# Conditioned residual pair on one core: all stores by pairs of 8 KB rows, loads left in fours

## The chip, the cores and the metric

The kernel runs on one core of one Trainium2 chip. The metric is the device time of one execution in microseconds (us). It is read as the median of several executions; profiles come from one more execution, which is recorded by the hardware profiler.

## The reference

There are 128 batches, each a matrix of 128 channels by 1024 time steps in float32. Two layers are applied to each. The first adds a product with one of 200 weight matrices, the second adds a product with one of 8 and a bias of 128 values:

```python
def _L0_cond_ref(x, conditions, weights):
    w = weights[conditions]
    return jnp.einsum('bct,bcd->bdt', x, w)
...
def _L1_cond_ref(x, subjects, weights, bias):
    w = weights[subjects]
    b = bias[subjects]
    out = jnp.einsum('bct,bcd->bdt', x, w)
    out = out + b[:, :, None]
    return out
x = x + _L0_cond_ref(x, itok_B_1_198, L0_cond_weights)
x = x + _L1_cond_ref(x, itok_B_0_7, L1_cond_weights, fside_8xS_0)
```

So out = (I + W1)^T (I + W0)^T x + b for each batch. The kernel reads x once and writes out once: 67.1 MB each way.

## The kernel before

The kernel forms one 128x128 matrix m = (I + W0)(I + W1) for each batch on TensorE, sums its parts on VectorE (`sum_m`), and multiplies it with x in two halves of 512 columns each (`results`). VectorE evicts the left half from PSUM with the bias added (`left`, line 378), ScalarE the right half (`right`, line 402). Both write back into the tile `xy`, over the x that has been used.

`xy` holds a ring of 8 slots. A slot is a pair of batches (2 x 1024 floats, 8 KB in each partition). Two slots make a "quad", four batches, and the ring holds four quads (QUAD = 2 slots, QUADS = 4). The 128 batches are 64 pairs, so the ring is filled 8 times (ROUNDS = 8). In DRAM, x and out are laid out by quads with the channel outermost: one channel of a quad is 16 KB in one piece, a channel of a pair is 8 KB of it.

The transfers of x and out are issued by SyncE (SP), in an order written out by hand, and all pass through the SP queue:

- at the start the first two pairs are loaded as pairs, then quads 1 to 3 (`load_quad`, lines 176 to 183), mixed with the loads of the first W0 matrices (64 KB each, rows of 512 B);
- `store_pair` stores slots 0 to 3 one by one, with `load_quad_again(1, 0)` among them (lines 188 to 192);
- then a loop (lines 193 to 199) has for each quad: the W0 loads of the quad after next (`load_w0_of`), the store of a finished quad (`store_quad`, line 156), and the load of a new one (`load_quad_again`, line 166), which first waits until the store that emptied its quad of the ring has landed. That store was issued one step of the loop earlier, so a store and a load are queued behind it whenever SP keeps up;
- the last part (lines 201 to 221) does the same without the loop, loads the last pair in smaller pieces, and stores quads 1 and 2 of the last round with `store_quad`, the pair after them with `store_pair`, and the last pair in halves of a batch, the left ones from SP, the right ones from ScalarE's queue (line 417).

`store_quad` waits in `wait_out` for the second pair of the quad, which is evicted after the first, and then issues one DMA of 2 MB. `store_pair` waits for its one pair and issues 1 MB. Each DMA adds 16 to the semaphore `stored[q]` of its quad. `stored_once(r, q)` is the value that says that quad q has been stored r times; for the first two quads it holds 16 more, since they were stored in two pieces in round 0. SP waits for it in `load_quad_again`, GpSimd ahead of `pick` (line 272; it copies the matrices of each batch from their home into the places that TensorE reads), and ScalarE at the end (line 420).

Of the kernel before, what the change touches and what calls it, by code (L numbers as in the profile page):

```python
# [11 lines left out]
def conditioned_residual_kernel(nc, x, cond, w0_t, w1_bias, out):  # L12
# [11 lines left out]
    NQ, C, QB, T = x.shape  # L24
    B = NQ * QB
    N0, _, D = w0_t.shape
    N1 = w1_bias.shape[1]
    assert C == D == 128
    PAIR = 2
    RING = 8  # L30
    QUAD = QB // PAIR
    QUADS = RING // QUAD
    PAIRS = B // PAIR
    ROUNDS = PAIRS // RING
# [3 lines left out]
    MB = 2  # L38
    YB = 2
    AHEAD = QUADS - 1  # L40
    BY_PAIR = 2
    assert PAIRS % RING == 0 and HALF <= 512 and RING % MB == 0 and ROUND_B % YB == 0

    with ExitStack() as ctx:
        def sb(name, shape, dt=F32):
            return ctx.enter_context(nc.sbuf_tensor(name, shape, dt))

        def sem(name):
            return ctx.enter_context(nc.semaphore(name))


        xy = sb("xy", [C, RING, PAIR, T])
# [35 lines left out]
        stored = [sem(f"stored{q}") for q in range(QUADS)]  # L88
# [12 lines left out]
        def half(h):  # L101
            return slice(h * HALF, (h + 1) * HALF)

        def slots(q):
            return xy[:, q * QUAD:(q + 1) * QUAD, :, :].rearrange("c s k t -> c (s k t)")

        def quad_of(t, r, q):
            return t[bass.ds(r * QUADS + q, 1), :, :, :].rearrange("n c k t -> (n c) (k t)")
# [3 lines left out]

        def stored_once(r, q):

            return r * 16 + (16 if q < BY_PAIR else 0)

        block = ctx.enter_context(nc.Block())

# [1 line left out]
        def _(sp):  # L120
# [29 lines left out]
            def wait_out(r, s):  # L150
                for k in range(PAIR):
                    b = s * PAIR + k
                    sp.wait_ge(left_out[b % YB], r * (ROUND_B // YB) + (b // YB + 1))  # L153
                    sp.wait_ge(right_out[b % YB], r * (ROUND_B // YB) + (b // YB + 1))  # L154

            def store_quad(r, q):

                wait_out(r, q * QUAD + QUAD - 1)
                sp.dma_start(quad_of(out, r, q), slots(q)).then_inc(stored[q], 16)  # L159

            def store_pair(r, s):
                wait_out(r, s)
# [3 lines left out]
            def load_quad_again(r, q):  # L166
                sp.wait_ge(stored[q], stored_once(r, q))
                load_quad(r, q)
# [24 lines left out]
            with sp.Fori(1, ROUNDS - 1) as r:  # L193
                for q in range(1, QUADS + 1):
                    now = (r, q) if q < QUADS else (r + 1, 0)
                    after = (r, q + 1) if q + 1 < QUADS else (r + 1, q + 1 - QUADS)
                    load_w0_of(*after)
                    store_quad(*((r, q - AHEAD) if q >= AHEAD else (r - 1, q - AHEAD + QUADS)))
                    load_quad_again(*now)

            for q in range(1, QUADS):
                if q < QUADS - 1:
                    load_w0_of(ROUNDS - 1, q + 1)
                store_quad(*((ROUNDS - 1, q - AHEAD) if q >= AHEAD else (ROUNDS - 2, q - AHEAD + QUADS)))
                if q < QUADS - 1:
                    load_quad_again(ROUNDS - 1, q)

            sp.wait_ge(stored[QUADS - 1], stored_once(ROUNDS - 1, QUADS - 1))
            load_pair(NQ - 1, LAST - 1, x_loaded[QUADS - 1])
            for k in range(PAIR):  # L210
# [3 lines left out]
            for q in range(1, QUADS - 1):  # L214
                store_quad(ROUNDS - 1, q)
# [10 lines left out]
        def _(pool):  # L226
            def pick(r, s):


                pool.wait_ge(w0_loaded[s], r * (PAIR * 16) + PAIR * 16)  # L230
                _, words = nc.values_load_multi_w_load_instructions(
                    pick_words[0:1, bass.ds(r * ROUND_B + s * PAIR, PAIR), :].rearrange("o b f -> o (b f)"),
                    engines=(mybir.EngineType.Pool,),
                    skip_runtime_bounds_check_because="each word is checked against its own range below")
                for k in range(PAIR):
                    home = nc.s_assert_within(words[2 * k], 0, B - 1)
                    i = nc.s_assert_within(words[2 * k + 1], 0, N1 - 1)
                    nc.gpsimd.tensor_copy(w0_pick[:, s, k, :],  # L238
                                          w0_home[:, bass.ds(home, 1), :].rearrange("k b c -> k (b c)"))
                    last = nc.gpsimd.tensor_copy(  # L240
                        j_pick[:, s, k, :], j_all[:, bass.ds(i, 1), :].rearrange("c n d -> c (n d)"))
                last.then_inc(picked, 1)

            def pick_first(s):


                _, words = nc.values_load_multi_w_load_instructions(
                    cond_words[0:1, 1, s * PAIR:(s + 1) * PAIR], engines=(mybir.EngineType.Pool,),
                    skip_runtime_bounds_check_because="each word is checked against its own range below")
                for k in range(PAIR):  # L250
                    i = nc.s_assert_within(words[k], 0, N1 - 1)
                    last = nc.gpsimd.tensor_copy(  # L252
                        j_pick[:, s, k, :], j_all[:, bass.ds(i, 1), :].rearrange("c n d -> c (n d)"))
                last.then_inc(picked, 1)
# [14 lines left out]
            with pool.Fori(1, ROUNDS) as r:  # L269
                for s in range(RING):  # L270

                    pool.wait_ge(stored[s // QUAD], stored_once(r, s // QUAD))
                    pick(r, s)
# [120 lines left out]
        @block.scalar  # L394
        def _(act):
            def right(r, s, k):

                b = s * PAIR + k
                if k == 0:
                    act.wait_ge(picked, r * RING + (s + 1))  # L400
                act.wait_ge(y_ready, r * (2 * ROUND_B) + (2 * b + 2))
                nc.scalar.activation(xy[:, s, k, half(1)], y_ps[:, b % YB, 1, :], ACT.Identity,  # L402
                                     bias=j_pick[:, s, k, D:D + 1]).then_inc(right_out[b % YB], 1)

            act.dma_start(cond_words[:].rearrange("o f b -> o (f b)"), cond).then_inc(cond_loaded, 16)
            with act.Fori(0, ROUNDS - 1) as r:
                for s in range(RING):
                    for k in range(PAIR):
                        right(r, s, k)
            for s in range(RING - 1):  # L410
                for k in range(PAIR):
                    right(ROUNDS - 1, s, k)
            for k in range(PAIR):
                b = LAST * PAIR + k
                right(ROUNDS - 1, LAST, k)
                act.wait_ge(right_out[b % YB], (ROUNDS - 1) * (ROUND_B // YB) + b // YB + 1)
                act.dma_start(out[NQ - 1, :, QB - PAIR + k, half(1)], xy[:, LAST, k, half(1)]).then_inc(last_stored, 16)
            for q in range(QUADS):

                act.wait_ge(stored[q], stored_once(ROUNDS, q))  # L420


# [23 lines left out]
```

## Time and profile before

| | |
|---|---|
| median of 3 runs | 347.63 us (347.43 to 348.22) |
| time of the profiled execution | 348.84 us |
| its span, first to last instruction | 347.1 us |
| busy share: TensorE matmul / VectorE / ScalarE / GpSimd | 77% / 36% / 28% / 19% |
| DMA packets, bytes, mean rate | 24058, 140.80 MB, 406 GB/s |
| share of 16 DMA engines taken by SP's queue | 97.9% |

Busy share is the time in which an engine ran instructions that count as work; the rate is what the 16 DMA engines of the core moved. "Issue to landing" is the time from SP's DMA instruction to the end of the whole transfer, with the time that it waited behind earlier ones.

### The profile page before, as it was taken

The page shows a single profiled execution, that of the slowest core. Times are in us where ns is not written, and L with a number is a line of the kernel's source. Part 1 is how long each engine was busy: PE and PEld are TensorE (multiplying, and loading weights), DVE is VectorE, ACT ScalarE, POOL GpSimd, SP SyncE. Part 2 cuts the span into 40 slices and gives each one's busy share as a digit, 9 for nine tenths or more (in the row PEclk, how much of TensorE's full clock was granted, in tenths as well). Part 3 has the DMA queues.
Part 4 walks back from the last instruction along what each step waited for, and adds up shares of the span by engine and source line. Part 5 has one row for each costly group of instructions (what it writes and reads, how often), then busy time and mean ns, then how long its engine had stood idle before and what let it go on. Part 6 is the DMA issues. An engine that isn't in the chain of part 4 may idle for free.

```text
span 347.1 us, 5157 instructions
## 1 busy us (share of the span) xinstructions
PE 266.8 (77%) x774; PEld 129.5 (37%) x774; DVE 126.3 (36%) x202; ACT 96.9 (28%) x135; POOL 65.3 (19%) x249
## 2 busy tenths in 40 slices
PE   1799991986798896979877779777679877778980
PEld 1344450442344442434433334433334433333430
DVE  3254541333334242433433344333334333334440
ACT  1133350221333133332232232422242222323230
POOL 2400222112221112221122212122221212221000
PEclk9999997899989898998999999999999999999996
DMA  7999969999999999999999999999999999999994
GB/s 306 410 409 393 378 248 351 424 418 397 417 431 415 433 423 427 417 416 427 432 425 427 427 423 432 421 436 423 419 431 425 432 430 426 423 421 440 419 405 171
DMA packets 24058, 140.80 MB, mean 406 GB/s; under 512 B 2673, under 2 KB 14322, under 8 KB 15474
## 3 DMA queue, kind: packets, MB, share of 16 engines
q1 hardware_dynamic: 23760, 140.20, 97.9%
q10 hardware_dynamic: 290, 0.53, 0.4%
q14 instruction: 7, 0.06, 0.0%
q8 instruction: 1, 0.02, 0.0%
HBM read 76.03 MB, written 67.11 MB: 412 GB/s over the span
## 4 chain that ended last, share of the span: by engine, by line
DMA 56%; SPq 27%; issue 9%; PE 5%; ACT 0%
DMA out<-xy 47%; SPq L127 10%; DMA xy<-x 9%; SPq L122 7%; PE y_ps L306 5%; SPq L128 4%; SPq L142 3%; SPq L145 2%; ACT xy L402 0%; PE m_ps L287 0%; SPq L159 0%; SPq L148 0%; SPq L153 0%; SPq L163 0%; SPq L154 0%
## 5 line engine op out<-in xcount | busy, mean ns | idle before, releaser
L306 PE MATMUL y_ps<-xy,m_sb 128*128 128x512 f32 x512 | 245.5, 616 | 61.3 <-DMA xy<-x 60.3
L306 PEld LDWEIGHTS y_ps<-xy,m_sb 128*128 128x128 f32 x512 | 92.9, 196 | 164.9 <-issue 164.9
L402 ACT ACTIVATE xy<-y_ps,j_pick 128x512 f32<-128x512 f32 x128 | 87.9, 687 | 233.1 <-PE y_ps L306 233.1
L378 DVE TENSOR_SCALAR xy<-y_ps,j_pick 128x512 f32<-128x512 f32 x128 | 96.1, 751 | 156.5 <-PE y_ps L306 156.5
L238 POOL COPY w_pick<-w_home 128x128 f32 x112 | 32.8, 293 | 245.4 <-issue 245.4
L287 PEld LDWEIGHTS m_ps<-j_pick,w_pick 128*128 128x128 f32 x224 | 35.4, 199 | 28.7 <-issue 28.7
L370 DVE TENSOR_TENSOR m_sb<-m_ps,j_pick 128x256 f32<-128x256 f32 x64 | 27.1, 424 | 45.2 <-PE m_ps L287 44.6
L287 PE MATMUL m_ps<-j_pick,w_pick 128*128 128x128 f32 x224 | 35.1, 281 | 0.0
L240 POOL COPY j_pick<-j_all 128x129 f32 x112 | 33.0, 295 | 0.1
L402 ACT ACT_TABLE_LOAD x7 | 9.0, 1283 | 7.9 <-POOL j_pick L252 7.8
L287 PE MATMUL m_ps<-j_pick,w_home 128*128 128x128 f32 x32 | 5.5, 297 | 6.7 <-DMA w_home<-w_t 6.7
L287 PEld LDWEIGHTS m_ps<-j_pick,w_home 128*128 128x128 f32 x32 | 5.3, 212 | 10.6 <-issue 10.4
L252 POOL COPY j_pick<-j_all 128x129 f32 x16 | 4.7, 295 | 10.3 <-issue 9.9
L312 PE MATMUL cond_ps<-cond_row,ones 1*128 1x128 f32 x2 | 0.8, 481 | 2.4 <-DVE cond_row L341 2.4
L344 DVE TENSOR_TENSOR j_all<-j_all,eye 128x1024 f32<-128x1024 f32 x1 | 1.2, 1226 | 2.3 <-DMA j_all<-w_bias 2.3
L361 DVE TENSOR_TENSOR load_words<-home_ps,batch_less_b 1x128 int32<-1x128 f32 x1 | 0.3, 278 | 4.7 <-PE home_ps L320 4.7
L312 PEld LDWEIGHTS cond_ps<-cond_row,ones 1*128 1x128 f32 x2 | 0.5, 309 | 2.4 <-issue 2.4
L341 DVE CAST cond_row<-cond_words 1x128 f32<-1x128 int32 x1 | 0.2, 214 | 2.1 <-DMA cond_words<-cond 2.1
L320 PE MATMUL home_ps<-eye,home_less_b 128*1 128x128 f32 x2 | 0.6, 394 | 0.0
L313 PEld LDWEIGHTS cond_ps<-ones,cond_row 1*128 1x128 f32 x2 | 0.5, 330 | 0.0
L313 PE MATMUL cond_ps<-ones,cond_row 1*128 1x1 f32 x2 | 0.4, 277 | 0.0
L351 DVE TENSOR_SCALAR same<-cond_ps,cond_col 128x128 f32<-128x128 f32 x1 | 0.4, 351 | 0.0
(16 smaller groups left out, 2.8 us busy)
## 6 DMA issues: line engine op xcount, KB each, us to landing
xy<-x SPq DMA_DIRECT2D x30, 2048.0 KB, 15.1
out<-xy SPq DMA_DIRECT2D x29, 2048.0 KB, 13.4
w_home<-w_t SPq DMA_DIRECT2D x128, 64.0 KB
out<-xy SPq DMA_DIRECT2D x5, 1024.0 KB, 6.8
xy<-x SPq DMA_DIRECT2D x3, 1024.0 KB, 7.8
xy<-x SPq DMA_DIRECT2D x4, 256.0 KB, 12.6
j_all<-w_bias SPq DMA_DIRECT2D x1, 516.0 KB, 3.7
out<-xy SPq DMA_DIRECT2D x2, 256.0 KB, 5.1
```

The source lines that it names most:

```text
L122: return nc.values_load_multi_w_load_instructions(words, engines=(mybir.EngineType.SP,), skip_runtime_bounds_check_because="each word is c ...
L127: sp.dma_start(w0_home[:, bass.ds(b, 1), :].rearrange("k b c -> k (b c)"), w0_t[bass.ds(nc.s_assert_within(i, 0, N0 - 1), 1), :, :].rearra ...
L128: w0_t[bass.ds(nc.s_assert_within(i, 0, N0 - 1), 1), :, :].rearrange("n k c -> (n k) c"),
L142: load_one(b + k, s, words[2 * k], nc.s_assert_within(words[2 * k + 1], 0, 1))
L145: sp.dma_start(slots(q), quad_of(x, r, q)).then_inc(x_loaded[q], 16)
L238: nc.gpsimd.tensor_copy(w0_pick[:, s, k, :], w0_home[:, bass.ds(home, 1), :].rearrange("k b c -> k (b c)"))
L240: last = nc.gpsimd.tensor_copy(j_pick[:, s, k, :], j_all[:, bass.ds(i, 1), :].rearrange("c n d -> c (n d)"))
L287: last = nc.tensor.matmul(m_ps[:, s % MB, k * D:(k + 1) * D], w0_of_k, j_pick[:, s, k, 0:D], start=True, stop=True)
L306: nc.tensor.matmul(y_ps[:, b % YB, h, :], m_sb[:, s, k, :], xy[:, s, k, half(h)], start=True, stop=True).then_inc(y_ready, 1)
L370: nc.vector.tensor_tensor(m_sb[:, s, :, :], m_ps[:, s % MB, 0:PAIR * D].rearrange("c (k d) -> c k d", k=PAIR), j_pick[:, s, :, 0:D], ALU.a ...
L378: nc.vector.tensor_scalar(xy[:, s, k, half(0)], y_ps[:, b % YB, 0, :], j_pick[:, s, k, D:D + 1], None, ALU.add).then_inc(left_out[b % YB], 1)
L402: nc.scalar.activation(xy[:, s, k, half(1)], y_ps[:, b % YB, 1, :], ACT.Identity, bias=j_pick[:, s, k, D:D + 1]).then_inc(right_out[b % YB ...
```

## The change

`store_quad` no longer issues one DMA of rows of 16 KB after the second pair is evicted. It goes through the two slots of its quad; for each it waits for that slot's pair and issues a DMA of 1 MB with rows of 8 KB. The semaphore of a quad now rises by 32 in each round, so `stored_once` becomes `r * 32` for every quad, and ScalarE's last wait is for 16 less on the last quad, whose last pair is stored in halves that count on another semaphore. Loads, the W0 loads, and the order of the issues are as before.

```diff
-    BY_PAIR = 2
...
         def stored_once(r, q):
 
-            return r * 16 + (16 if q < BY_PAIR else 0)
+            return r * (QUAD * 16)
...
             def store_quad(r, q):
 
-                wait_out(r, q * QUAD + QUAD - 1)
-                sp.dma_start(quad_of(out, r, q), slots(q)).then_inc(stored[q], 16)
+                for s in range(q * QUAD, (q + 1) * QUAD):
+                    wait_out(r, s)
+                    sp.dma_start(out[bass.ds(r * QUADS + q, 1), :, (s % QUAD) * PAIR:(s % QUAD + 1) * PAIR, :]
+                                 .rearrange("n c k t -> (n c) (k t)"),
+                                 xy[:, s, :, :].rearrange("c k t -> c (k t)")).then_inc(stored[q], 16)
...
             for q in range(QUADS):
 
-                act.wait_ge(stored[q], stored_once(ROUNDS, q))
+                act.wait_ge(stored[q], stored_once(ROUNDS, q) - (16 if q == QUADS - 1 else 0))
```

## Rows read from the trace of the kernel before

**Rows 1.** The page: 40 slices of DMA share (tenths) and rate; SP's queue.
```profile
DMA  7999969999999999999999999999999999999994
GB/s 306 410 409 393 378 248 351 424 418 397 417 431 415 433 423 427 417 416 427 432 425 427 427 423 432 421 436 423 419 431 425 432 430 426 423 421 440 419 405 171
...
q1 hardware_dynamic: 23760, 140.20, 97.9%
```

**Rows 2.** DMA issues: transfer, issuing queue, count, KB each, median us from issue to landing.
```profile
xy<-x SPq DMA_DIRECT2D x30, 2048.0 KB, 15.1
out<-xy SPq DMA_DIRECT2D x29, 2048.0 KB, 13.4
...
out<-xy SPq DMA_DIRECT2D x5, 1024.0 KB, 6.8
```

**Rows 3.** SP's waits, 60 to 300 us: total us, times, longest; none other there.
```profile
SPq L145 <- DMA out<-xy: 55.6, 23, 3.5
```

**Rows 4.** Timeline of SP, two steps of the loop: start us, us, line, transfer.
```profile
74.17 0.35 SPq L159 DMA_DIRECT2D out<-xy  x1
77.71 0.35 SPq L145 DMA_DIRECT2D xy<-x  x1
80.01 4.96 SPq L127 DMA_DIRECT2D w_home<-w_t  x4
85.40 0.35 SPq L159 DMA_DIRECT2D out<-xy  x1
88.17 0.35 SPq L145 DMA_DIRECT2D xy<-x  x1
```

**Rows 5.** Timeline of ACT there: the last eviction of one quad.
```profile
79.72 0.69 ACT L402 ACTIVATE xy<-y_ps,j_pick 128x512 f32<-128x512 f32 x1 [1.48 <-PE y_ps L306]
```

**Rows 6.** Windows: stretch, us, five engines' busy time, granted clock, DMA share, GB/s.
```profile
0.00:28.00 28.00, 17.89 (x51) 9.42 (x52) 9.99 (x21) 5.41 (x7) 5.76 (x25) 1.00 0.95 369
...
28.00:34.00 6.00, 6.00 (x22) 3.13 (x21) 3.06 (x6) 2.06 (x3) 0.00 (x0) 1.00 1.02 422
...
30.00:34.00 4.00, 4.00 (x14) 1.98 (x13) 2.04 (x4) 1.37 (x2) 0.00 (x0) 1.00 1.02 424
...
200.00:300.00 100.00, 78.46 (x237) 37.72 (x236) 38.12 (x60) 30.05 (x42) 20.46 (x78) 1.00 1.01 427
...
306.00:318.00 12.00, 9.53 (x32) 4.72 (x31) 4.77 (x8) 3.40 (x5) 2.12 (x8) 1.00 1.04 433
...
312.00:322.00 10.00, 7.51 (x25) 3.60 (x24) 3.85 (x6) 2.75 (x4) 2.12 (x8) 1.00 0.99 424
```

**Rows 7.** Chain of work, first store of the loop: start us, us, line.
```profile
47.43 0.06 SPq L153
...
47.83 0.36 SPq L159
```

**Rows 8.** Timeline of SP at the start of the loop, and windows there.
```profile
26.88 1.88 SPq L163 DMA_DIRECT2D out<-xy  x3
...
57.15 0.35 SPq L159 DMA_DIRECT2D out<-xy  x1
...
46.00:48.00 2.00, 2.00 (x9) 1.21 (x8) 0.75 (x1) 1.97 (x3) 1.06 (x4) 1.00 0.13 38
```

**Rows 9.** The end: SP's waits from 300 us, timelines of SP and ACT, windows.
```profile
SPq L153 <- DVE xy L378: 14.0, 3, 9.1
...
320.22 10.83 SPq L159 DMA_DIRECT2D out<-xy  x2
...
326.06 0.69 ACT L402 ACTIVATE xy<-y_ps,j_pick 128x512 f32<-128x512 f32 x1 [1.42 <-PE y_ps L306]
...
326.00:328.00 2.00, 2.00 (x9) 1.04 (x8) 0.75 (x1) 0.69 (x1) 0.00 (x0) 1.00 1.16 483
...
330.00:332.00 2.00, 2.00 (x9) 1.12 (x8) 0.75 (x1) 0.91 (x2) 0.00 (x0) 1.00 0.94 396
...
342.00:344.00 2.00, 0.00 (x0) 0.00 (x0) 0.00 (x0) 0.00 (x0) 0.00 (x0) 0.50 0.12 49
```

## The prediction

> **What bounds the kernel now.** I read the slices of the page first [rows 1]. From the seventh slice to the last but one the DMA share stands at nine tenths or more, and the rate at 397 to 440 GB/s from the eighth on, while TensorE is busy for 77% of the span and no other engine for more than 36%. SP's queue alone took 97.9% of the time of 16 DMA engines. So the transfers are the bound; the reader should see that there is one real hole in the middle (slice 6, at 248 GB/s) and a thin last slice (171). The issues come second [rows 2]: a 2 MB load lands 15.1 us after its issue and a 2 MB store 13.4 us after, though 2 MB at 427 GB/s [rows 6] take only 4.9 us. The rest is waiting behind earlier transfers: about 4 MB lie ahead of each. Third come SP's own waits [rows 3]: between 60 and 300 us it waits only at line 145, for the landing of the store that frees a quad, 23 times, 2.4 us each. Its timeline [rows 4] shows the same: store issued at 85.40, then idle until the store of 74.17 has landed, load at 88.17. A step takes 88.17 - 77.71 = 10.5 us, which is 4.19 MB of x and out and up to 0.26 MB of W0 at 427 GB/s (10.4 us). SP is paced by the transfers, not the transfers by SP.
>
> **Part 1, the wait is split so that a pair can leave earlier.** In the loop this moves nothing. The quad that SP stores at 85.40 [rows 4] had its last eviction at 79.72 + 0.69 = 80.41 us [rows 5], 5.0 us before. SP arrives late because it issues W0 loads from 80.01 to 84.97. Both pairs are long evicted, and the two DMAs will go out back to back. None of SP's waits from 60 to 300 us is for an eviction [rows 3]. Value 0, and no gain in the loop, since even a store issued earlier would stand in a queue that is full.
>
> **Part 2, the price of the extra issue on SP.** The first store of the loop shows the whole step [rows 7]: from 47.43 us (the first wait's register work) to 48.19 us (the end of the issue), 0.76 us, with the address arithmetic. The change adds one such step to each quad store, about 0.8 us. It stands ahead of the wait for landing at line 145, which has 2.4 us of idle time in the mean [rows 3] and some 2.3 us in the step shown (85.75 to about 88.0) [rows 4]. Cover: that idle time. Behind SP are queued the load and the next W0 loads; neither is delayed, as the landing of the older store sets the load's issue. The second half of a store gets into the queue 0.8 us later, with some 10 us of transfers ahead of it. Value 0. If the cover were gone it would be 24 x 0.8 = 19 us in the loop. The loads' own wait is for the same bytes as before, in the same place in the queue; the higher count at lines 145, 272 and 420 moves nothing.
>
> At the start of the loop there is less cover. The queue runs dry at 46 to 48 us (38 GB/s, share 0.13) [rows 8], because SP is late, and stays thin until the next store at 57.15 us. The dry spell itself ends with the first store, which still goes out at about 47.8 us, and its 1 MB (2.5 us at 422 GB/s) covers the 0.8 us until the second. The next store would then be at 57.15 + 0.8 = 58.0 us. From about 48.1 us the queue holds 4.19 + 0.26 = 4.45 MB, 10.5 us, so until 58.6 us. It just holds, with 0.6 us to spare. The bounds are 0 and one step of SP, 0.8 us (no gain is possible where SP arrives late); I take a quarter of the step, **+0.2 us**, as the margin is as small as the step.
>
> **Part 3, the rows of 8 KB.** This is the term that matters, as it sits on the bound itself. There are 29 quad stores [rows 2], so 29 x 2.097 = 60.8 MB go by 8 KB rows: 29 x 128 = 3712 rows of 16 KB become 7424, and 29 more DMAs complete. The trace has one stretch that is made of such stores and nothing else. By 26.9 us SP had issued the joint table (0.5 MB), two pairs (2.1), three quads (6.3) and up to 20 W0 matrices (1.3), together 10.2 MB; 28 us at 369 GB/s are 10.3 MB [rows 6]. So at 28 us those are done, and the three 1 MB stores issued from 26.88 to 28.76 [rows 8] are what moves from 28 to 34 us: 422 GB/s at a share of 1.02 [rows 6]. The hundred microseconds of the loop, all 16 KB rows but for the W0, move 427 GB/s [rows 6]. Then 60.8 MB take 60.8 / 0.422 = 144.1 us in place of 60.8 / 0.427 = 142.4 us: **+1.7 us**. The 28 to 34 stretch holds three completions, so they are in that price. Bounds: the shorter cut 30 to 34 (424) against the stretch 312 to 322 (424), where no W0 is left: 0. And 422 against 306 to 318 (433): 144.1 - 140.4 = +3.7 us. I take 1.7, from the two longest and cleanest windows, though W0 rows slow the 427 a little, which speaks for more rather than less.
>
> Here the Trainium skill has a rule that speaks against the change. "DMA: Bandwidth & Descriptors", section "Why small descriptors are slow (HBM only)", gives each packet three cycles on top of one per 32 bytes. By that 8 KB cost 259 and 16 KB 515 cycles, so two halves 518 for 515, 0.6% of 142 us; an estimate of +0.8 us by that page, and the sum would be 1.0 us in place of 1.9. The trace's own rates ask for somewhat more.
>
> **Part 4, the end.** Here SP does wait for evictions, 14.0 us in 3 waits [rows 9]: before the stores of the last round. The store at 331.05 - 0.35 = 330.7 us (quad 2, the second of the two at 320.22 [rows 9]) could send its first pair when ScalarE has evicted it, at 326.06 + 0.69 = 326.75 us: 1 MB leaves SP 3.9 us earlier. But the engines are full all that time: 483 GB/s at 326 to 328 us, 396 at 330 to 332, shares 1.16 and 0.94 [rows 9]. What is issued earlier only queues earlier. Value 0. Below nothing the bound is the time that the last engines work nearly alone: from 342 us the share is 0.12 [rows 9], for some 3 us to the end, a tail that another order could shorten by at most 3 us. On the other side an extra issue of 0.8 us before the last stores. There I take 0 all the same, as SP is waiting for an eviction ahead of each of these stores and has the time.
>
> **Sum.** 0 (part 1) + 0.2 (part 2) + 1.7 (part 3) + 0 (part 4) = 1.9 us. On the profiled execution that is 348.84 + 1.9 = 350.7 us (span 347.1 + 1.9 = 349.0). The profiled execution lies 1.2 us above the median of the runs, which is what counts: 347.63 + 1.9 = **349.5 us**.
>
> **The rivals.**
> (a) *No change.* The rows of 8 KB move at the rate of 16 KB ones, as the pair 424 and 424 says [rows 6], and everything else is covered: 347.6 us, 347.0 to 348.3. A 6 us window is short, and in its favour is that a few GB/s is what single windows differ by. Against it: the DMA share is full, so nothing hides even a small price.
> (b) *Faster.* The end has slack of its own: the early first pair of quad 2 (3.9 us ahead) and of quad 1 in the last round fills some engines that would otherwise be empty, and the stretch of thin work after 342 us shrinks. It gives up to 3 us less the 1.7 us, so about 346.3 us. It decides only if some engines run dry before 331 us; the shares of 1.16 and 0.94 speak against that.
> (c) *Much slower: SP becomes the bound.* If the added step costs more than the 2.4 us of cover [rows 3], or the queue empties once again after 57 us and does not refill, each dry step costs up to 0.8 us. Four of them before the queue is full again are 3.2 us, which with the 1.7 is 347.63 + 4.9 = 352.5 us. It decides when the queue's 10.5 us of bytes fall short of SP's step.
> (d) *Each DMA has a fixed part that isn't hidden.* A 1 MB store lands 6.8 us after its issue [rows 2] with at most two such stores (5.0 us) ahead of or in it, so 1.8 us is fixed. If that were on the path 29 times it would be 52 us, 400 us in all. The stretch of three in a row at 422 GB/s rules it out almost wholly. The Trainium skill, same page, section "Bandwidth", has figures of this kind (transfers of 1 MB issued from GpSimd reach 341 GB/s, of 16 MB 425); the trace's 422 GB/s at 1 MB, queued from SP, disagrees.
>
> **How the numbers follow.** About 0.2% (0.7 us) is what a measurement of this kernel can tell from no change. The forecast (cost of 0.7 to 3.7 us, 348.3 to 351.3) has 0.62, (a) 0.20, (b) 0.12, (c) 0.05, (d) 0.01. Slower is the forecast with (c) and (d), 0.68; same is (a), 0.20; faster is (b), 0.12. The range goes from 347.0, the lower end of (a), to 351.3, the upper end of the forecast, 0.82 by these cases.
>
> **What would show it.** Packets rise by 3712 rows and 29 x 16 = 464 completions to about 28,230, at the same 140.8 MB; the rate from 200 to 300 us falls from 427 to some 423 to 425 GB/s at an unchanged share; SP's wait at line 145 (its new number) shrinks from 2.4 to about 1.6 us each; two store issues stand 0.8 us apart in each step, both after the evictions; the hole before the first store of the loop stays as it is; in the last round one store leaves near 327 + 2 us and changes nothing. I am wrong if the rate in the loop does not fall, if the hole at 46 us widens or a second one appears after 57 us, or if the thin stretch at the end changes its length by over a microsecond.

## The result and the profile after

| | before | changed |
|---|---|---|
| median of 5 runs | 347.63 us (347.41 to 348.22) | 350.74 us (350.16 to 351.35) |
| ratio, 95% interval | | 1.0086 (1.0067 to 1.0105) |
| profiled execution, span | 348.84 us, 347.1 us | 351.13 us, 349.3 us |

The changed kernel is 3.1 us slower; by the interval 2.3 to 3.7 us. The page of its profile, with the same lines as [rows 1] and the span and packets with them:

```profile
span 349.3 us, 5304 instructions
...
DMA  7999969999999999999999999999999999999984
GB/s 306 412 401 394 356 243 363 436 417 426 407 420 420 426 432 419 417 418 426 421 433 429 416 425 425 423 421 434 431 417 425 424 429 422 432 420 421 415 335 185
DMA packets 28235, 140.81 MB, mean 403 GB/s; under 512 B 3137, under 2 KB 14786, under 8 KB 15938
...
q1 hardware_dynamic: 27936, 140.20, 97.6%
```

The same bytes go in 4177 more packets; the hole in slice 6 is as it was (243 for 248 GB/s), the loop's slices are alike, and the last slice but one is thinner: 335 for 405 GB/s. The issues, to be held against [rows 2] (columns as there):

```profile
out<-xy SPq DMA_DIRECT2D x63, 1024.0 KB, 9.6
xy<-x SPq DMA_DIRECT2D x30, 2048.0 KB, 15.0
```

SP's one wait from 60 to 300 us (as [rows 3]), and its timeline at the start of the loop and in two later steps (as [rows 4]; line 159 is the store, line 144 the load):

```profile
SPq L144 <- DMA out<-xy: 38.5, 20, 3.0
...
48.28 1.08 SPq L159 DMA_DIRECT2D out<-xy  x2
49.57 1.11 SPq L144 DMA_DIRECT2D xy<-x  x1
...
58.15 1.07 SPq L159 DMA_DIRECT2D out<-xy  x2
59.42 1.16 SPq L144 DMA_DIRECT2D xy<-x  x1
...
68.35 1.07 SPq L159 DMA_DIRECT2D out<-xy  x2
69.63 0.84 SPq L144 DMA_DIRECT2D xy<-x  x1
...
106.84 1.07 SPq L159 DMA_DIRECT2D out<-xy  x2
110.47 0.35 SPq L144 DMA_DIRECT2D xy<-x  x1
```

Two stores stand where one stood and take 1.08 us together, 0.73 more than one. The wait behind them has shrunk as it should, over the 23 loads of the stretch; but three of these loads found no wait at all. In the changed kernel the first five loads of the loop (49.57 to 89.82 us) leave 0.2 us behind the stores, in the kernel before only the first two (48.46 and 57.70 us). And the load takes SP 1.11 and 1.16 us in the first steps, where one of before took 0.34 to 0.35 [rows 4]. Windows, columns as in [rows 6], first of the changed kernel, then two that the section of rows did not need, of the kernel before:

```profile
0.00:60.00 60.00, 44.20 (x130) 22.72 (x130) 22.70 (x41) 16.31 (x22) 11.97 (x48) 0.99 0.92 354
60.00:110.00 50.00, 40.36 (x106) 19.58 (x107) 16.59 (x26) 12.97 (x18) 8.85 (x34) 0.88 1.02 422
...
200.00:300.00 100.00, 79.46 (x240) 38.31 (x239) 38.21 (x60) 29.37 (x41) 20.31 (x76) 1.00 1.01 425
...
324.00:328.00 4.00, 3.90 (x9) 2.24 (x10) 0.75 (x1) 0.69 (x1) 0.00 (x0) 0.61 1.02 399
345.00:348.00 3.00, 0.00 (x0) 0.00 (x0) 0.00 (x0) 0.00 (x0) 0.00 (x0) 0.55 0.07 26
```

```profile
0.00:60.00 60.00, 43.44 (x130) 22.20 (x130) 22.70 (x41) 16.31 (x22) 12.19 (x49) 0.98 0.92 355
60.00:110.00 50.00, 41.35 (x117) 20.24 (x118) 18.08 (x28) 13.93 (x20) 8.54 (x33) 0.93 1.02 419
```

Two things are to be seen. In the loop the rate is 425 for 427 GB/s. And by 110 us the changed kernel has moved no less than the one before: 0.354 x 60 + 0.422 x 50 = 42.34 MB for 0.355 x 60 + 0.419 x 50 = 42.25 MB. Yet its load of that time is issued at 110.47 us, the other's at 109.07. A load goes out when the whole of an older store has landed, so it waits for the last of the 16 DMA engines, and the mean rate does not show that one. The last window shows it alone: 26 GB/s at a share of 0.07 is one engine of 16 at full speed (427 / 16 = 26.7), still at work three microseconds after the others.

The trace shows the same within the loop, as it has the time of each of the 16 additions to a semaphore. For the load issued at 88.17 us (89.82 in the changed kernel) the fifteenth comes at 103.35 us before and at 103.11 us in the changed kernel, the last at 103.62 and at 105.07 us: it trails by 0.3 and by 2.0 us. In the second profile of each, below, it trails by 0.0 and by 2.6 us.

**Where the time went.** The starts of the loads of x are the clock of this kernel, so they date the loss. Each column is one profiled execution; the second of each kernel comes from the experiments below.

| load issued, us | before | before again | changed | changed again | means differ by |
|---|---|---|---|---|---|
| first after the pair stores | 34.16 | 33.83 | 34.91 | 33.85 | +0.4 |
| first of the loop | 48.46 | 48.34 | 49.57 | 49.02 | +0.9 |
| seventh of the loop | 109.07 | 108.52 | 110.47 | 110.45 | +1.7 |
| last quad | 306.24 | 305.75 | 307.87 | 307.75 | +1.8 |
| last pair | 316.82 | 316.30 | 319.04 | 318.92 | +2.4 |
| end of the span | 347.1 | 346.6 | 349.3 | 349.3 | +2.5 |

The 0.4 us at 34 us lies ahead of the first changed instruction and is chance. Of the other 2.1 us, 0.5 arise at the first doubled store, 0.8 in the next 60 us, 0.1 in the 200 us after that, and 0.6 between the last two loads. Three experiments below came out as the kernel before once more. Against the mean of all five such profiles the last column reads +0.3, +0.8, +1.8, +2.2, +2.8 and +2.8 us, so the 200 us of the loop lose 0.4 us and not 0.1.

### The profile page after: what moved, and what is told of

Same layout as the page of the kernel before. It is cut to its first block, busy times and chain, and to the rows that moved or that the text cites. A ratio compares the mean times of both kernels' runs of the same rounds, so it can differ in the third digit from the quotient of the medians.

```text
span 349.3 us, 5304 instructions
## 1 busy us (share of the span) xinstructions
PE 269.9 (77%) x774; PEld 131.1 (38%) x774; DVE 126.2 (36%) x202; ACT 97.0 (28%) x135; POOL 65.7 (19%) x249
## 2 busy tenths in 40 slices
DMA packets 28235, 140.81 MB, mean 403 GB/s; under 512 B 3137, under 2 KB 14786, under 8 KB 15938
## 4 chain that ended last, share of the span: by engine, by line
DMA 59%; SPq 21%; PE 9%; issue 8%; DVE 1%; ACT 1%
DMA out<-xy 34%; DMA xy<-x 25%; PE y_ps L308 8%; SPq L126 7%; SPq L121 5%; SPq L127 3%; SPq L141 2%; SPq L159 2%; SPq L144 2%; PE m_ps L289 1%; DVE xy L380 1%; ACT xy L404 1%; SPq L152 0%; SPq L147 0%; SPq L165 0%
## 5 line engine op out<-in xcount | busy, mean ns | idle before, releaser
L289 PEld LDWEIGHTS m_ps<-j_pick,w_pick 128*128 128x128 f32 x224 | 36.2, 203 | 29.9 <-issue 29.9
L289 PE MATMUL m_ps<-j_pick,w_pick 128*128 128x128 f32 x224 | 35.9, 285 | 0.0
```

Of the source, the lines that this page charges most:

```text
L289: last = nc.tensor.matmul(m_ps[:, s % MB, k * D:(k + 1) * D], w0_of_k, j_pick[:, s, k, 0:D], start=True, stop=True)
```

## The experiments

All ratios are to the kernel before, run beside each kernel on the same chip. The microseconds behind a ratio are that ratio of some 347.8 us; medians subtracted from each other can differ from them by half a microsecond. Most lines of an edit that only follow from those shown are left out.

**The changed kernel again.** No edit.

> The changed kernel once more, unaltered, for a second profile and a second ratio. Theory R (the price lies on the rows of 8 KB, spread evenly over the loop, about 1.7 us): ratio near 1.005 to 1.009, and from the issue at 109 us to that at 307 us the loads of x fall behind the kernel before by over 1.0 us. Theory S (the price lies at the two ends of the program, where SP is late at the start of the loop and where the last quads are computed, and the loop itself costs nearly nothing): same ratio, but over those 19 quads the loads fall behind by under 0.4 us, and from the last loads to the last eviction by over 1.0 us. If the first profile's hole at 338 us and TensorE's clock of 0.50 at 326 us were chance, they are gone here and the span is shorter by 1 to 2 us.

Measured: 350.50 us, ratio 1.0064 (1.0041 to 1.0086), +2.2 us; span 349.3. From the load near 109 us to that near 307 us its lag on the first profile of before went from 1.38 to 1.51 us: 0.13 us over 19 quads (0.23 in the first profile), as S said and not R. That test is weaker than it looks: five profiles of the kernel before take 196.3 to 197.2 us for these quads, and the two of the changed kernel 197.4 and 197.3. The 1.0 us that S put behind the last loads isn't there. The late last product of the first profile was chance. The chain of the second, and the timeline of the first, at the quad after the last full load:

```profile
323.98 1.96 PE y_ps L308 x4
```

```profile
324.11 3.02 PE L308 MATMUL y_ps<-xy,m_sb 128*128 128x512 f32 x4 [3.14 <-DMA xy<-x]
```

In the first, TensorE had idled 3.14 us and ran at a granted clock of 0.61 in the mean from 324 to 328 us (a mix of its two levels, 1.2 and 2.4 GHz), so its last eviction began at 341.13 us, in the second at 339.33. Both spans are 349.3. The end is set by the last DMA engine, not by the last product.

**Pairs in the loop alone.**

Against the changed kernel; the counts of `stored_once` follow, and GpSimd's last round is taken out of its loop:

```diff
+    IN_LOOP = 2
+    AFTER_LOOP = 1
...
-            def store_quad(r, q):
-
+            def store_quad(r, q, n=AFTER_LOOP):
+                if n == 1:
+                    wait_out(r, q * QUAD + QUAD - 1)
+                    sp.dma_start(quad_of(out, r, q), slots(q)).then_inc(stored[q], 16)
+                    return
                 for s in range(q * QUAD, (q + 1) * QUAD):
...
-                    store_quad(*((r, q - AHEAD) if q >= AHEAD else (r - 1, q - AHEAD + QUADS)))
+                    store_quad(*((r, q - AHEAD) if q >= AHEAD else (r - 1, q - AHEAD + QUADS)), n=IN_LOOP)
```

> Stores by pairs only in the 24 quads of SP's loop; the five quads stored behind the loop go as one DMA of 2 MB each again. GpSimd's last round is taken out of its loop so that the counts can differ. Theory R: 24/29 of the cost stays, +2.6 us of the measured +3.1. Theory S: what is left is the start of the loop, +0.5 to +1.4 us, and the last stretch from the loads of the last pair to the end is as in the kernel before (no share under 0.8 between 330 and 340 us). Rival N (the end is set by noise in when the last loads land, whatever form the stores have): ratio as the changed kernel's.

Measured: 350.59 us, ratio 1.0063 (1.0044 to 1.0082), +2.2 us (1.5 to 2.8). With 24 of the 29 quads the whole of the cost is there within the intervals. R's +2.6 us lies in the interval, S's +0.5 to +1.4 us does not; from 330 to 340 us no window of 2 us falls under a share of 0.89, as S said. But the profile of this kernel is 0.8 us late before any store (its load at 6.7 us goes out at 7.54), and if all its executions are, that is part of its 2.2 us.

**Pairs behind the loop alone.** The same code with `IN_LOOP = 1` and `AFTER_LOOP = 2`.

> Stores by pairs only in the five quads stored behind SP's loop; the 24 in the loop go as one DMA of 2 MB each. GpSimd's last round is taken out of its loop as well. Theory R: 5/29 of the cost, +0.5 us, ratio 1.001 to 1.002. Theory S: +1.0 to +2.0 us, ratio 1.003 to 1.006, with the last eviction more than 1 us later than in the kernel before although the loads up to 306 us are issued at the same times as there (within 0.4 us).

Measured: 348.74 us, ratio 1.0025 (1.0006 to 1.0044), +0.9 us (0.2 to 1.5). Small, but not nothing. The profile can't place it, since the profiled execution took 351.28 us, the slowest of the kernel's twelve, and it too is late from the start (7.60 for 6.72 us). R's +0.5 us lies in the interval, S's upper half does not; the last eviction is late (339.05 us), but the load at 306 us of before is late by 1.81 us there as well, so that test of S could not be made.

**Two DMAs with rows of 16 KB.**

```diff
-                sp.dma_start(quad_of(out, r, q), slots(q)).then_inc(stored[q], 16)
+                for p in (slice(0, C // 2), slice(C // 2, C)):
+                    sp.dma_start(out[bass.ds(r * QUADS + q, 1), p, :, :].rearrange("n c k t -> (n c) (k t)"),
+                                 xy[p, q * QUAD:(q + 1) * QUAD, :, :].rearrange("c s k t -> c (s k t)"))\
+                      .then_inc(stored[q], 16)
```

> All 29 quads are stored in two DMAs of 1 MB as in the changed kernel, but cut by partitions (64 and 64) with rows of 16 KB, both issued after the second pair is evicted. So the second issue and the second completion stay, and the rows of 8 KB and the early first pair are gone. Theory R: the cost goes, ratio 0.999 to 1.002. Theory S with SP's second issue as the cause at the start: the loads at 59 and 69 us are late as in the changed kernel (1.7 and 3 us behind before), and at least +1 us stays. If it is slower than the changed kernel, 64 partitions use the engines less evenly, and it tells nothing of rows.

Measured: 376.88 us in the median of five executions, ratio 1.0827 (1.0777 to 1.0876), +29 us; the profiled one took 382.81 us, the longest. It answers another question: two DMAs of 64 partitions take longer here than one of 128, with the same rows. Its page and its loop:

```profile
DMA packets 24523, 140.81 MB, mean 370 GB/s; under 512 B 3137, under 2 KB 14786, under 8 KB 15938
...
200.00:300.00 100.00, 77.76 (x218) 37.53 (x217) 34.91 (x55) 27.30 (x38) 19.12 (x72) 0.94 1.00 389
```

The share is full at 389 GB/s, so packets took longer: rows of 16 KB 667 ns in the mean of this stretch, for 612 before. It tells nothing of the change.

**The kernel before again.** No edit.

> The kernel before, unaltered, as a second profile: how far two executions of the same program stand apart stage by stage. If its loads are issued within 0.3 us of the first profile's, then the +1.4 us by which the changed kernel's loads are late at 109 us is the change's; if they differ by 1 us, the start varies by itself and less can be read from it. Ratio 1.000 within 0.002.

Measured: 347.85 us, ratio 0.9991 (0.9972 to 1.0011). Its loads stand 0.1 to 0.6 us from those of the first profile (table above). So differences under about half a microsecond between two profiles say nothing (under one microsecond, with the three further profiles below), and the changed kernel's 1.7 us at 109 us does.

**GpSimd's loop cut, nothing else.** The control for the two kernels with pairs in one part.

```diff
-            with pool.Fori(1, ROUNDS) as r:
+            with pool.Fori(1, ROUNDS - 1) as r:
+                pick_round(r)
+            pick_round(ROUNDS - 1)
```

> The kernel before with only GpSimd's last round taken out of its loop, as the two kernels with pairs in one part had it. Both had their second load of x 0.8 to 0.9 us late already at 6.7 us, ahead of any store. If the longer GpSimd program is the cause, it shows here too: loads at 6.7 to 34 us late by 0.8 to 1.4 us, and a ratio of 1.001 to 1.003, which has to be taken off theirs: the pairs in the loop then cost 0.4 to 0.6%, and the pairs behind it 0 to 0.2%. If not, it is 1.000.

Measured: 347.83 us, ratio 0.9997 (0.9979 to 1.0014); its loads up to 16 us are within 0.02 us of before's. The cut costs nothing by itself. But the late start of the two kernels above (there SP waited 0.9 and 1.0 us for its index words) isn't here, so this control does not cover it. Whether it was in all their executions, and so in their ratios, is open. The 0.9 us of the pairs behind the loop could be mostly that.

**One DMA with rows of 8 KB, first try.**

```diff
-                sp.dma_start(quad_of(out, r, q), slots(q)).then_inc(stored[q], 16)
+                sp.dma_start(out[bass.ds(r * QUADS + q, 1), :, :, :].rearrange("n c (s k) t -> (n c) s (k t)", s=QUAD),
+                             xy[:, q * QUAD:(q + 1) * QUAD, :, :].rearrange("c s k t -> c s (k t)"))\
+                  .then_inc(stored[q], 16)
```

> Each quad is stored by one DMA once both pairs are evicted, as in the kernel before, but its access pattern is split so that a row is 8 KB: the rows of the change without its second issue, second completion and early first pair. Packets near 27,800. Theory R (rows): ratio 1.005 to 1.008. Theory S (SP's second issue delays the start, the tail does the rest): 0.999 to 1.002.

Measured: 347.89 us, ratio 0.9997 (0.9980 to 1.0013), but the packets line shows that the edit did not take:

```profile
DMA packets 24058, 140.80 MB, mean 406 GB/s; under 512 B 2673, under 2 KB 14322, under 8 KB 15474
```

24058 is the number of before. The two pieces, adjoining on both sides, were joined to rows of 16 KB. It is one more run of the kernel before.

**SP's time alone.**

```diff
                 sp.dma_start(quad_of(out, r, q), slots(q)).then_inc(stored[q], 16)
+                words_of(load_words[0:1, 0:PAIR, :].rearrange("o b f -> o (b f)"))
```

> The kernel before, with one more read of index words into SP's registers behind each quad store (0.5 to 0.9 us of SP's time, nothing else): SP's added time of the change alone, without rows or DMAs. Theory S: the loads at 59 to 70 us fall 1 to 3 us behind, and the ratio is 1.003 to 1.006. Theory R: the wait for the landing at the load swallows it, ratio 0.999 to 1.001.

Measured: 347.78 us, ratio 1.0000 (0.9983 to 1.0017), and this too is void: the profile holds 5157 instructions, as before. The words are not used, so the read was presumably dropped. SP's time by itself stays untried.

The two void kernels serve as further profiles of the kernel before; with the first two and that of the cut loop there are five. Their loads near 109 us stand at 107.99 to 109.40 us, those of the last quad at 305.09 to 306.24 us. The changed kernel's, at 110.46 and 307.81 us in the mean, lie 1.1 and 1.6 us behind the latest of them. Their rate from 200 to 300 us is 426 to 428 GB/s, the changed kernel's 425 in both profiles: a small fall, but a real one (summed packet by packet, 42.67 to 42.73 MB for 42.54 and 42.50).

**Rows of 8 KB in all loads and stores, no further issue.**

```diff
-        xy = sb("xy", [C, RING, PAIR, T])
+        xy_wide = sb("xy", [C, RING, PAIR * T + 64])
+        xy = xy_wide[:, :, 0:PAIR * T].rearrange("c s (k t) -> c s k t", k=PAIR)
...
-            return xy[:, q * QUAD:(q + 1) * QUAD, :, :].rearrange("c s k t -> c (s k t)")
+            return xy[:, q * QUAD:(q + 1) * QUAD, :, :].rearrange("c s k t -> c s (k t)")
...
-            return t[bass.ds(r * QUADS + q, 1), :, :, :].rearrange("n c k t -> (n c) (k t)")
+            return t[bass.ds(r * QUADS + q, 1), :, :, :].rearrange("n c (s k) t -> (n c) s (k t)", s=QUAD)
```

> The kernel before with 256 B of room behind each pair in the ring of x, so that the 16 KB of a quad are no longer one piece in SBUF: each of its rows has to go as two of 8 KB, in loads and stores alike, still one DMA for each quad. Packets near 31,600, no second issue, no second completion. It carries twice the rows of the change. Theory R (8 KB rows cost 1.7 us for the stores): +3.5 us or more, ratio near 1.010. Theory S (rows cost nearly nothing in the loop; the changed kernel's loads fell behind there by only 0.13 and 0.23 us over 19 quads): 0 to +1 us, ratio under 1.003.

Measured: 351.73 us, ratio 1.0100 (1.0080 to 1.0120), +3.5 us (2.8 to 4.2). The edit took this time (packets), and SP's issues grew a little longer with it, from 0.35 to 0.6 us:

```profile
DMA packets 31611, 140.80 MB, mean 402 GB/s; under 512 B 2674, under 2 KB 14323, under 8 KB 15475
...
78.55 0.64 SPq L160 DMA_DIRECT2D out<-xy  x1
79.47 0.60 SPq L146 DMA_DIRECT2D xy<-x  x1
```

Twice the rows of the change cost what R said. Half of it, 1.7 us (1.4 to 2.1), would be the stores' part if loads and stores weigh alike. The time that the DMA engines were at work gives the price without the ratio. It stands on the pages, as SP's queue's share of the span; of the changed kernel's second profile, and of this kernel:

```profile
q1 hardware_dynamic: 27936, 140.20, 97.7%
```

```profile
q1 hardware_dynamic: 31312, 140.20, 97.9%
...
200.00:300.00 100.00, 78.23 (x238) 37.99 (x238) 37.37 (x59) 29.67 (x42) 20.14 (x76) 1.00 1.02 424
```

Before, 97.9% of 347.1 us are 339.8 us for each engine. In the changed kernel it is 340.9 and 341.3 us, here 343.0 us: 1.1 to 1.5 us for the rows of the stores, completions included, and 3.2 us for those of all quads. Single packets agree: most rows of 16 KB take 611 ns and most of 8 KB 309 ns, so two halves take 7 ns more, and 3712 x 7 ns / 16 engines = 1.6 us. The remaining rows of 16 KB were not slower in the changed kernel (619 and 620 ns in the mean, for 618 to 620 in the five profiles of before). The rate of the loop falls with it, 427 before, 425 changed, 424 here.

The starts of the loads are a poorer measure. At 34 us they are already 1.49 us late (35.65 for 34.16), from first loads which the change leaves alone, and from the first load of the loop (50.22 for 48.46, +1.76) to that of the last quad (309.36 for 306.24, +3.12) they fall behind by 1.36 us over 25 loads and as many stores: 0.8 us for 29 stores, 1.4 against the fastest of the five profiles of before. So the rows of the change are worth some 1.1 to 1.6 us, and at most 2.1.

**One small DMA more behind each quad store.**

```diff
+            def one_more(q):
+                sp.dma_start(spare[:, q, :], w0_t[0, 0:16, :]).then_inc(spared[q], 16)
...
                 sp.dma_start(quad_of(out, r, q), slots(q)).then_inc(stored[q], 16)
+                sp.wait_ge(spared[q], r * 16 + (16 if q >= 2 else 0))
+                one_more(q)
...
                 store_pair(0, s)
+            for q in range(QUADS):
+                one_more(q)
             load_quad_again(1, 0)
```

> The kernel before, with one more small DMA (16 partitions of 512 B into a spare tile) issued behind each of the 29 quad stores, and four at the start for its counts: the second issue and the second completion of the change without its rows. Theory S (SP's longer step, which starts the loop late): loads at 59 to 70 us 1 us or more behind, ratio 1.003 to 1.007. Theory R: ratio 0.999 to 1.002. In both cases the 0.24 MB that it adds are worth under 0.1%.

Measured: 350.50 us, ratio 1.0082 (1.0064 to 1.0101), +2.9 us (2.2 to 3.5), more than S asked for, though the interval reaches into its range, and far from R's nothing. It has no row of 8 KB that before hasn't, and 0.27 MB more (0.6 us at 427 GB/s, 0.19% and not the "under 0.1%" of the expectation), in rows of 512 B. Those are slow for their size: 528 rows of 27 ns and as many completions of 9 ns are 1.2 us for each of 16 engines. That leaves 1.0 to 2.3 us for the further issue itself, and it is the price of one more small load, which need not be that of a second store. Its timeline at the start of the loop (line 159 is the small DMA):

```profile
57.76 0.35 SPq L164 DMA_DIRECT2D out<-xy  x1
58.16 0.42 SPq L159 DMA_DIRECT2D spare<-w_t  x1
58.78 1.16 SPq L147 DMA_DIRECT2D xy<-x  x1
...
68.95 0.34 SPq L147 DMA_DIRECT2D xy<-x  x1
```

The long load issue is here too (1.16 us), and the loads are as late as in the changed kernel: 58.78 and 68.95 for 57.70 and 66.54 us. In this execution the delay was made up by 109 us (108.89 for 109.07). But the profiled execution was the fastest of its six (349.71 us; the others 350.25 to 351.63), so where the others lost 1 to 2 us more can't be read.

**The store ahead of the W0 loads.**

```diff
-                    load_w0_of(*after)
                     store_quad(*((r, q - AHEAD) if q >= AHEAD else (r - 1, q - AHEAD + QUADS)))
+                    load_w0_of(*after)
                     load_quad_again(*now)
```

> The kernel before with the store of a quad moved ahead of the W0 loads in each step of SP's loop. The store of round 0's quad 2 then goes out near 42 us in place of 47.8, and the hole at 44 to 48 us should close by most of its 3.5 us. Both theories: faster, 1 to 3 us, ratio 0.991 to 0.997, unless the W0 loads, now later, hold up GpSimd's copies.

Measured: 347.24 us, ratio 0.9975 (0.9960 to 0.9990), 0.9 us (0.3 to 1.4) faster than before and the best version here, though less than the 1 us that was the least expected. Windows of it, and three of before to compare:

```profile
43.00:48.00 5.00, 5.00 (x19) 2.71 (x18) 2.42 (x5) 2.96 (x4) 0.65 (x3) 1.00 1.04 439
...
48.00:52.00 4.00, 4.00 (x14) 1.99 (x13) 2.05 (x4) 1.76 (x3) 1.47 (x6) 1.00 0.86 272
...
0.00:60.00 60.00, 44.73 (x132) 23.01 (x133) 22.72 (x41) 16.31 (x22) 12.19 (x49) 0.97 0.98 375
...
300.00:320.00 20.00, 16.76 (x45) 8.32 (x44) 6.84 (x11) 4.81 (x7) 3.84 (x15) 0.83 1.00 404
320.00:340.00 20.00, 16.38 (x48) 7.65 (x46) 8.15 (x13) 6.18 (x9) 0.41 (x2) 1.00 0.97 399
```

```profile
48.00:52.00 4.00, 4.00 (x13) 1.97 (x12) 1.99 (x4) 1.78 (x3) 1.06 (x4) 1.00 0.99 410
...
300.00:320.00 20.00, 16.00 (x48) 7.71 (x48) 7.71 (x12) 5.36 (x8) 3.95 (x15) 1.00 1.02 429
320.00:340.00 20.00, 15.31 (x44) 7.34 (x44) 7.28 (x11) 5.63 (x9) 1.06 (x4) 1.00 0.99 413
```

The hole at 44 to 48 us is closed, but the 4 us behind it are thinner than before (272 for 410 GB/s). In the first 60 us 20 GB/s more are 1.2 MB, 2.8 us at 427 GB/s. Between 300 and 340 us 25 and 14 GB/s less, over 20 us each, are 0.78 MB: 1.8 us given back. There the share is full or nearly so and the packets are slower; why is open.

**The same with pairs.** The changed kernel with the same move.

> The changed kernel with the same move. Here SP waits for evictions in the loop, and a first pair can leave before the second. Theory S: with the store out early at the start of the loop, SP's second issue no longer delays it, and the kernel comes within 1 us of the one before with the same move. Theory R: it stays 1.7 to 3 us slower than that one.

Measured: 350.12 us, ratio 1.0062 (1.0040 to 1.0083), +2.2 us on before and 2.9 us over its twin with quads (350.12 - 347.24). S had it within 1 us, so S as it was put falls: without the hole at 44 to 48 us the cost of pairs is as large. The start is not cleared by that, though. Two windows, to be held against those of the twin above:

```profile
48.00:52.00 4.00, 4.00 (x15) 2.09 (x14) 1.94 (x4) 1.76 (x4) 1.11 (x5) 1.00 0.64 211
...
0.00:60.00 60.00, 44.17 (x130) 22.72 (x130) 22.71 (x41) 16.31 (x22) 12.19 (x49) 0.99 0.95 363
```

The thin stretch has only moved, and with pairs it is thinner (211 for 272 GB/s). The first 60 us move 363 for 375 GB/s, 0.72 MB less, which is 1.7 us at 427 GB/s; the loads are late by 1.4 us at 49 us (50.93 for 49.49) and by 2.8 us at 57 us (59.97 for 57.22), and the two spans differ by 1.9 us. So in these profiles most of what the pairs cost here arises in the first 60 us, where SP is late.

## Why the prediction was right

The forecast was 349.5 us, +1.9 us; +3.1 us were measured in the first runs, +2.2 in the second, within the range and on the forecast's side. The large term, the rows, is borne out in mechanism and about in size. One small term was far too small, and that the sum held all the same owes something to luck. Point by point:

- **What bounds the kernel.** Right: the rate and the share of the DMA engines stayed full and the time moved with what they were given. What the argument missed is that a mean over 16 engines is not the bound. The last engine is: equal bytes at 110 us stand beside loads 1.4 us late, and the last of the 16 additions trails by 2.0 and 2.6 us in the changed kernel where it trailed by 0.3 and 0.0. What drives one engine back is open. Pairs alone don't: over the loads that land from 90 to 200 us it trails by 2.0 and 2.8 us in the mean in the two profiles of the changed kernel, by 0.2 to 0.5 in the five of before, and by 0.8 and 0.7 with pairs in the loop alone and with pairs and the store moved ahead, which cost as much as the changed kernel's second measurement.
- **Part 1**, no gain in the loop from an earlier first pair: right. Both stores go out back to back (1.08 us for two), behind the evictions.
- **Part 2**, SP's step. Its price was right (0.76 us put, 0.73 measured) and so was its cover in the steady loop: the wait at the load fell from 55.6 us to 38.5 us, from 2.4 to 1.7 us for each of 23 loads, as forecast. The term that failed is the start, +0.2 us. "It just holds, with 0.6 us to spare" counted one longer step. The load's issue grew as well, from 0.35 to 1.1 us, and the delay added up over two steps: the third load of the loop came 3.1 and 2.5 us late (69.63 and 69.06 for 66.54), and 1.4 us were left at 109 us. SP found no wait at the load in five steps, where before it was two. By the table the loads lose 1.3 us from the first doubled store to 109 us, a few tenths of it for the rows, where the term had 0.2. A further small DMA without rows of 8 KB cost 2.9 us (2.2 to 3.5), 1.2 of it for its own packets.
- **Part 3**, the rows of 8 KB, +1.7 us: about right. The engines' own time gives 1.1 to 1.5 us, the single packets 1.6, half of the kernel with twice the rows 1.4 to 2.1; the lower estimate in the prediction, 0.8 us, is below all of them. The way to the number was less sure than it looked. The stretch of 28 to 34 us, ahead of all changed code, reads 416 to 422 GB/s over the seven profiles of the two kernels, and the loop of before 426 to 428. So the difference is real, but the prediction took the top of the first range, and it held stores alone against loads and stores.
- **Part 4**, the end at 0: pairs behind the loop alone cost 0.9 us (0.2 to 1.5), of which their rows are 0.2 to 0.3. Whether the rest is the end's, or a late start, is not shown. The early first pair left at 330.71 us in the first profile (328.91 in the second), hardly before the whole quad of before (330.7), and brought nothing, as forecast; the queue then ran thin, which is the 335 GB/s of the last slice but one (389 in the second profile).
- **The sum** came out near because its large term held and the microsecond missing at the start is small beside a range that is 3 us wide; that part is luck. Half of the kernel with twice the rows is 1.7 us, and a further issue, less its packets, is 1.7 us too. The change has both and costs 2.2 to 3.1 us, somewhat less than their sum, but within the intervals of the two.
- **The signs** came: 28235 packets, a loop at 425 GB/s, waits down by 0.7 us, stores 0.73 us apart, the hole as it was. A fall of 2 GB/s says something only because the five profiles of before all lie at 426 to 428.

Of the rivals, (a), (b) and (d) are out by the measured sign and size. (c) had the right place for the missing part, SP's step at the start of the loop, but its rule "each dry step costs" was wrong: no stretch ran dry that had not before.

**Still open.** How the second issue costs time while the share of the engines is full; where the 1.7 us of the small DMA lie that its own packets don't explain; and why one engine falls behind. SP's time alone was not tried, as the edit for it was void.

## What to carry to other kernels

On a kernel whose transfers fill the DMA engines, cutting a 2 MB store in two buys nothing when the issuer arrives after both parts are ready, and that the issuer has time to spare does not make the further issue free: here a small DMA added behind each of 29 stores cost about 0.1 us apiece, 0.04 of it for its packets. The smaller rows cost some 0.05 us for each 2 MB. Read the loads' issue times of several profiles of each kernel side by side before a loss is given to a mechanism: the mean rate hid a loss of 1.4 us that they showed, and they in turn differ by a microsecond between profiles of one program, where the engines' own time differs by half of one. And look where the issuer is late for work that is long ready: moving one store ahead of small loads was worth more than any cut of it.

## What the runs showed that was not expected

- One DMA engine of the 16 ends last: at the end of the kernel before it works alone for some 2 us, in the changed one for 3 (26 GB/s, share 0.07 from 345 to 348 us). Of the stores by 64 partitions alone this isn't so.
- A row of 16 KB took an engine 611 ns and a row of 8 KB 309 ns, so halving a row cost 7 ns.
- SP's issue of a 2 MB load took 1.1 us in place of 0.35 behind two other DMAs issued at once, but only in the first steps of the loop (1.11, 1.16, 0.84, 0.52, 0.41 us, then 0.35 again).
- Stores of 64 partitions with rows of 16 KB, two for each quad, held the loop to 389 GB/s and cost 29 us.
- Pieces of an access pattern that adjoin on both sides are joined: without room between them the rows stayed at 16 KB, with 256 B of it they were 8 KB.
